# The bias of an attention's output projection: added by TensorE as three bf16 rows, not by GpSimd

## The chip, the cores and the metric

The kernel runs on one NeuronCore of a Trainium2 chip. The metric is the device time of one execution in microseconds (us); shown is the median of three runs. Five engines work side by side and meet only at semaphores: TensorE (PE, with PEld for its weight loads), VectorE (DVE), ScalarE (ACT), GpSimd (POOL) and SyncE (SP, which issues DMAs).

## What is computed

The input is `x` of 16 images by 4 groups by 128 tokens by 256 features, in float32. Three layers follow one another:

```
h = token_mix(x)                       # softmax weights over the 4 groups, weighted sum: 16 x 128 x 256
a = layernorm(h)
q, k, v = a @ W_qkv.T + b_qkv          # 16 heads of 16
p = softmax(causal(q @ k.T) / sqrt(16))
h = h + (p @ v) @ W_o.T + b_o          # the bias in question is b_o
n = layernorm(h)
h = h + moe(n)                         # 64 experts, 6 of them per token, and a shared expert
```

The bias of `v` passes through the softmax unchanged, because the probabilities of a row sum to one. So the kernel adds it as one joint row, `b_o + b_v @ W_o.T`, after the projection. That joint row is what `bo_sb` holds, the same on all 128 partitions.

## The kernel before

The work is tiled by image: 128 tokens lie on the 128 partitions, 256 features in a row. The whole of `h` stays in SBUF as `h_all` (128 x 16 x 256). The program is written out engine by engine. `image_loop` runs a `step(b, par)` on PE, DVE, ACT and POOL for b from -2 or -1 up to 17 or 18, and each step is a software pipeline in which the engines handle different images: image b+3 is mixed and normed by DVE (`a` there; PE and ACT take image b+2 as their `a`), image b+1 gets its V projection, image b its scores and softmax, image b-1 (`cc`) its output projection, residual and second norm, images b-2 (`d`) and b-3 (`e`) their routing to experts and the writing of their rows to DRAM. The order of instructions on each engine is written by hand; every wait is a semaphore. After the loop comes the expert stage, tile by tile (`tile_loop`), and the summing of its results; the change doesn't touch these.

What matters for one step of the loop:

- PE, in its order: `scores()` of image b, the turn of the attention output, V projection (image b+1), transposes, `turn_shift()`, the output projection of image `cc` (line 1252, two products of f32, each run in two passes, into columns 256 to 511 of the bank `psC`), `keyed()` scores, the QKV projection of image b+2, and the products with V (`pv`). All products go through the helper `mm`, so the profile puts them on L1064; the tile names tell them apart.
- DVE, in its order: the first half of the row maxima (`nmax`, L702), the softmax's denominator, the first mixing product, the normalising of the attention output, the second half of `nmax`, `shift_b` (L710, L712), three more mixing instructions (L692), interleaved with the placing (`slot_ix`, L799) and routing (`gsel`, L757) of earlier images, then the residual add of the projection (L905), the norms' statistics, and `apply` (L696), which writes `xn` for the attention or six copies of the normed row for the experts.
- POOL, in its order: the bias add for image b+1 (L406), which waits until DVE has normed that image, the reciprocal root for the norms (`roots`, L381 and L383), and six indirect DMAs that scatter the rows of image b-3 (L398).

The residual add L905 waits for the projection (`proj_done`) and for POOL's bias add of the same image (`bias_added`). Ahead of the loop, DVE mixes and norms images 0 and 1, and its last instruction there, L965, joins the bias and tells POOL (`bias_joined`). `ones_b` is a 128 x 128 tile of bf16 ones that the kernel already uses as stationary operand when it counts rows per expert (L1215). `const_sb` is one table of constants, made on the host and loaded with one DMA.

Of the kernel before, what the change touches and what calls it, by code (L numbers as in the profile page):

```python
# [13 lines left out]
P = 128  # L14
# [36 lines left out]

_at = 0
C_AT = {}
for _name, _n in (("ident", P), ("tri", P), ("tri_t", P), ("pick", GH), ("before", P), ("half", 2), ("ebase", E),
                  ("dest", NB * TOPK), ("spill", 1 + NY), ("upto", E), ("tile", NTAB)):
    C_AT[_name] = (_at, _n)
    _at += _n
# [9 lines left out]
def build(nc, x, w1t, b1, w2t, b2, wqkv, bqkv, wo, bo, gate, gbias, sgu, sd, wexp, const, out):  # L67
# [4 lines left out]
    with ExitStack() as ctx:  # L72
        def sb(name, shape, dt=F32):
            return ctx.enter_context(nc.sbuf_tensor(name, shape, dt))
# [28 lines left out]
        bv_wide = sb("bv_wide", [P, KT, P])  # L103
        wo_sb = sb("wo_sb", [P, KT, D])
        bo_sb = sb("bo_sb", [P, D])
        gate_sb = sb("gate_sb", [P, KT, E])
        gbias_sb = sb("gbias_sb", [P, E])
        gbias_half = sb("gbias_half", [P, E])
# [114 lines left out]
        for name in ("consts_ready", "sum_act", "sum_dve", "tok_chain", "tok_hid", "tok_tanh",  # L223
                     "tok_h", "bv_spread", "bv_projected", "bias_joined", "tok_w", "tok_shift", "tok_exp",
                     "mix_chain", "ln1_done", "xn_transposed", "xnt_ready", "qk_done", "q_ready", "k_ready",
                     "qk_bias", "v_done", "v_ready", "scores_done", "shift_parts", "shift_ready", "shift_turned",
                     "shift_copied", "keyed_done", "exp_done", "pv_done", "ot_ready", "ot_turned", "c2_chain", "o_ready",
                     "o_transposed", "ont_ready", "bias_added", "proj_done", "ln_chain", "x2_ready", "var_ready", "root_ready", "var_eps", "half_set",
                     "x2_transposed", "x2t_ready", "gate_done", "gate_tanh", "g_chain", "score_read", "sel_ready",
                     "pos_done", "key_read", "d_chain", "pool_step", "gu_done", "gu_silu", "sh_chain", "counted",  # L230
                     "shared_done", "h2_ready", "row_ready", "t_chain", "t_count", "t_cum", "t_past", "t_rows",
                     "tab_ready", "xt_done", "xt_ready",
                     "up_done", "silu_done", "h_ready", "h_turned", "ht_ready", "down_done", "pads_zero", "pads_ready", "y_ready",
                     "fin_half", "fin_pair", "fin_ready"):
            S(name)
# [35 lines left out]
        def has(b, lo=0, hi=NB - 1):  # L271
            return not isinstance(b, int) or lo <= b <= hi
# [100 lines left out]
        def _(pool):  # L373
# [16 lines left out]
                roots(n, n + 1, n + 1)  # L390
            pool.wait_ge(S("bias_joined"), 1)

            def step(b, par):
                v, e = b + 1, b - 3

                def scatter(choices):
                    for k in choices:
                        nc.gpsimd.indirect_dma_start(  # L398
                            out=slots_dram,
                            out_offset=bass.IndirectOffsetOnAxis(ap=slot_ix[:, e % NROW, k:k + 1], axis=0),  # L400
                            in_=row_of(e)[:, k, :], in_offset=None).then_inc(scattered[e % NROW], 16)

                if has(v):

                    pool.wait_ge(S("ln1_done"), v + 1)
                    nc.gpsimd.tensor_tensor(h_all[:, v, :], h_all[:, v, :], bo_sb[:], ALU.add).then_inc(  # L406
                        S("bias_added"), 1)
                ahead = TAIL_AHEAD if b == NB else 0
                if ahead:
                    pool.wait_ge(S("row_ready"), e + 1)  # L410
                    scatter(range(ahead))
                if -2 < b <= NB:
                    pool.wait_ge(S("var_ready"), b + 4 if b < 0 else 2 * b + 4 if b <= 12 else b + 16)
                    roots(0 if has(b + 3) else 1, 2 if has(b - 1) else 1, b + 4)
                if has(e):
                    pool.wait_ge(S("row_ready"), e + 1)
                    pool.sem_inc(S("pool_step"), 1)
                    scatter(range(ahead, TOPK))
# [166 lines left out]
        def _(dve):  # L585
# [245 lines left out]
            def step(b, par):  # L831
# [69 lines left out]
                routed(3)  # L901
                if has(cc):
                    dve.wait_ge(S("proj_done"), cc + 1)
                    dve.wait_ge(S("bias_added"), cc + 1)
# [157 lines left out]
        def _(pe):  # L1062
            def mm(*a, **k):
                return nc.tensor.matmul(*a, **k)  # L1064
# [55 lines left out]
            def step(b, par):  # L1120
# [128 lines left out]
                if has(cc):  # L1249
                    pe.wait_ge(S("ont_ready"), cc + 1)  # L1250
                    wait(pe, S("x2_ready"), cc)
                    both(psC[:, D:2 * D], lambda k: ont[:, k, :], lambda k: wo_sb[:, k, :]).then_inc(
                        S("proj_done"), 1)
                if has(b):
                    keyed()
                if has(a):
# [177 lines left out]
```

## Time and profile before

| | |
|---|---|
| median of three runs | 505.59 us (505.51, 505.59, 508.94) |
| profiled execution | 508.18 us, of which 506.4 us lie between its first and its last instruction |
| busy in that span | PE 435.2 us, PEld 335.3, DVE 321.7, POOL 245.9, ACT 215.6 |
| bias adds on POOL (L406) | 16, the first at 25.5 us, the last at 208.6 us |
| first `nmax` of the loop, first one after it | 34.10 us, 48.23 us |

In the tables of the profile PE's time is that of its matrix products, whose ends are modelled. A row of the timeline gives the start in us, the duration in us, the engine, the line, the operation, the tile written and the tiles read, the shape, and how many instructions of a kind are merged in the row; in brackets stands how long the engine was idle before it, and what ended that.
### The profile page before, as it was taken

The numbers are of one execution on the slowest core, as the hardware profiler recorded it, in microseconds if no ns is written. First come the engines' busy times: TensorE is split into PE (matmuls) and PEld (weight loads), VectorE is DVE, ScalarE is ACT, GpSimd is POOL, SyncE is SP. The second block draws the span as 40 slices with busy tenths as digits, with TensorE's granted clock in tenths as the row PEclk, the third lists the DMA queues.
The fourth block names the chain that finished last, engine by engine and source line by source line (L and its number), as shares of the span: only waits on it lengthen the run. The fifth ranks groups of instructions, "written<-read, shape, count | busy, mean of one in ns | idle before, by whom it ended". The sixth has DMA issues, their size and how long they took to land. (4 is left out here: it accounts for less than half of the span.)

```text
span 506.4 us, 13166 instructions
## 1 busy us (share of the span) xinstructions
PE 435.2 (86%) x3950; PEld 335.3 (66%) x3950; DVE 321.7 (64%) x1065; ACT 215.6 (43%) x662; POOL 245.9 (49%) x273
## 2 busy tenths in 40 slices
PE   1667889888989999778369999999999999985995
PEld 1556667676767777454148887888888888862663
DVE  3674789999899998967713443444444444440998
ACT  3254755564545655332004454454444445440000
POOL 1111115766666678766713655665556565661000
PEclk9988999998989999987769999999999999996999
DMA  7999991212111111222235678568577757744997
GB/s 269 337 351 262 277 257 56 72 60 74 65 64 66 64 65 68 83 85 74 104 105 166 194 233 260 173 200 260 174 216 246 226 138 224 212 136 171 377 370 274
DMA packets 56476, 90.00 MB, mean 178 GB/s; under 512 B 7719, under 2 KB 43690, under 8 KB 56400
## 3 DMA queue, kind: packets, MB, share of 16 engines
q1 hardware_dynamic: 44016, 61.69, 40.3%
q0 software_dynamic: 10080, 25.29, 14.0%
q10 hardware_dynamic: 2304, 2.10, 1.2%
q8 instruction: 37, 0.61, 0.6%
q14 instruction: 39, 0.32, 0.2%
HBM read 84.00 MB, written 40.82 MB: 246 GB/s over the span
## 5 line engine op out<-in xcount | busy, mean ns | idle before, releaser
L428 POOL DMA_INDIRECT y_rows<-y,xring x114 | 112.1, 984 | 91.5 <-issue 81.1
L1064 PE MATMUL ps_low<-wring,probt 128*128 x456 | 119.4, 385 | 0.0
L1025 DVE TENSOR_TENSOR probt<-probt,ps_low 128x128 f32<-128x128 f32 x114 | 32.8, 288 | 110.3 <-issue 90.1
L1064 PEld LDWEIGHTS ps_low<-wring,probt 128*128 128x128 f32 x456 | 78.8, 193 | 6.5 <-issue 0.2
L1064 PE MATMUL ps<-wring,probt 128*128 x228 | 68.4, 382 | 0.0
L565 ACT COPY probt<-ps_low 128x256 f32<-128x256 f32 x115 | 42.8, 372 | 50.3 <-PE ps_low L1310 48.7
L398 POOL DMA_INDIRECT slot_rows<-row,slot_ix x48 | 51.5, 1072 | 15.7 <-issue 13.1
L1018 DVE TENSOR_SCALAR y<-ps,xring 128x256 f32<-128x256 f32 x114 | 54.6, 479 | 6.8 <-DMA y_rows<-y,xring 5.3
L398 POOL DMA_INDIRECT slot_rows<-xring,slot_ix x48 | 51.4, 1070 | 14.0 <-issue 13.7
L570 ACT ACTIVATE probt<-ps_low 128x128 f32<-128x128 f32 x114 | 31.7, 278 | 58.1 <-PE ps_low L1064 57.5
L480 ACT ACTIVATE probt<-ps_low 128x512 f32<-128x512 f32 x64 | 33.1, 602 | 43.1 <-PE ps_low L1064 43.1
L1310 PE MATMUL ps_low<-const_sb,xring 128*128 128x128 f32 x230 | 44.9, 277 | 4.2 <-DMA xring<-slot_rows 4.0
L702 DVE TENSOR_REDUCE nmax<-ps_low 128x8 f32<-128x1024 f32 x32 | 39.0, 1217 | 9.3 <-PE ps_low L1064 9.2
L1310 PEld LDWEIGHTS ps_low<-const_sb,xring 128*128 128x128 f32 x230 | 32.5, 143 | 17.4 <-issue 5.1
L381 POOL TENSOR_SCALAR rv<-mv 128x2 f32<-128x2 f32 (+1 forms) x20 | 4.5, 222 | 80.7 <-DVE mv L849 68.3
L1064 PEld LDWEIGHTS ps<-wring,probt 128*128 128x128 f32 x228 | 34.4, 191 | 8.7 <-issue 0.3
L1064 PE MATMUL ps_low<-x_sb,sgu_sb 128*128 128x512 f32 x64 | 32.9, 664 | 7.0 <-issue 7.0
L1064 PE MATMUL ps<-xnt,wqkv_sb 128*128 128x128 f32 x256 | 36.2, 300 | 0.5 <-ACT xnt L513 0.5
L1064 PEld LDWEIGHTS ps<-xnt,wqkv_sb 128*128 128x128 f32 x256 | 33.0, 209 | 3.3 <-issue 2.6
L1297 PE MATMUL ps<-const_sb,probt 128*128 128x128 f32 x114 | 31.3, 275 | 0.8 <-DVE probt L1025 0.8
L559 ACT COPY probt<-ps 128x128 f32<-128x128 f32 x114 | 29.6, 260 | 1.4 <-PE ps L1297 1.3
L1064 PEld LDWEIGHTS ps_low<-x_sb,sgu_sb 128*128 128x128 f32 x64 | 13.5, 216 | 22.9 <-issue 22.6
(184 smaller groups left out, 739.8 us busy)
## 6 DMA issues: line engine op xcount, KB each, us to landing
wring<-wexp SPq DMA_DIRECT2D x115, 384.0 KB
xring<-slot_rows SPq DMA_DIRECT2D x115, 129.0 KB, 2.6
x_sb<-y_rows SPq DMA_DIRECT2D x16, 768.0 KB, 7.0
slot_rows<-pads SPq DMA_DIRECT2D x1, 8256.0 KB
x_sb<-x SPq DMA_DIRECT2D x3, 2048.0 KB, 17.8
slot_rows<-pads SPq DMA_DIRECT2D x5, 516.0 KB
x_sb<-x SPq DMA_DIRECT2D x4, 512.0 KB, 5.3
out<-h_all ACTq DMA_DIRECT2D x16, 128.0 KB, 6.7
```

Of the source, the lines that this page charges most:

```text
L398: nc.gpsimd.indirect_dma_start(out=slots_dram, out_offset=bass.IndirectOffsetOnAxis(ap=slot_ix[:, e % NROW, k:k + 1], axis=0), in_=row_of( ...
L428: nc.gpsimd.indirect_dma_start(out=y_dram, out_offset=bass.IndirectOffsetOnAxis(ap=xring[:, q, TO_AT:TO_AT + 1].bitcast(I32), axis=0), in_ ...
L480: nc.scalar.activation(probt[:, g].rearrange("p a k -> p (a k)"), psQ[g][:], ACT.Exp).then_inc(S("exp_done"), 1)
L559: nc.scalar.copy(ht[:, v % 2, :], ps[4 + v % 2][:, 0:P]).then_inc(S("ht_ready"), 1)
L565: nc.scalar.copy(xt[:, u % 2].rearrange("p a k -> p (a k)"), psT[u % 2][:, 0:D]).then_inc(S("xt_ready"), 1)
L570: nc.scalar.activation(silu[:, t % 2, :], psS[t % 2][:, 0:INTER], ACT.Silu).then_inc(S("silu_done"), 1)
L702: nc.vector.tensor_reduce(nmax[:, two, :], ps_low[:, two, :].rearrange("p g (a k) -> p g a k", a=GH), axis=AX, op=ALU.max, negate=True).th ...
L1018: nc.vector.tensor_scalar(y[:, a, :], ps[6 + v % 2][:, 0:D], xring[:, v % U, W_AT:W_AT + 1], None, ALU.mult).then_inc(S("y_ready"), 1)
L1025: nc.vector.tensor_tensor(hm[:, t % 2, :], silu[:, t % 2, :], psS[t % 2][:, INTER:2 * INTER], ALU.mult).then_inc(S("h_ready"), 1)
L1064: return nc.tensor.matmul(*a, **k)
L1297: nc.tensor.transpose(ps[4 + v % 2][:, 0:P], hm[:, v % 2, :], ident).then_inc(S("h_turned"), 1)
L1310: last = nc.tensor.transpose(psT[u % 2][:, k * P:(k + 1) * P], xring[:, uq, k * P:(k + 1) * P], ident)
```

## The change

POOL's bias adds in the loop are gone, and with them the semaphore `bias_added` on both sides. Ahead of its loop POOL now splits the joint bias into three bf16 terms by ten instructions in a chain: three copies to bf16, two differences in float32, three products with a mask that keeps partition k of term k alone (the new three columns `term` of the constants), and two sums that put the three rows into one tile, `bo_rows`: row 0 holds the first term, row 1 the second, row 2 the third, and the other partitions zero. On PE, each output projection now begins its accumulation with a bf16 product of `ones_b` and `bo_rows`, which adds up the three rows for every token; the two f32 products accumulate on top. Before the first one PE waits once for `bias_rows`. DVE's residual add stays as it is and waits for the projection alone.

```
--- before.py
+++ after.py
@@ -51,7 +51,7 @@
 
 _at = 0
 C_AT = {}
-for _name, _n in (("ident", P), ("tri", P), ("tri_t", P), ("pick", GH), ("before", P), ("half", 2), ("ebase", E),
+for _name, _n in (("ident", P), ("tri", P), ("tri_t", P), ("pick", GH), ("before", P), ("half", 2), ("term", 3), ("ebase", E),
                   ("dest", NB * TOPK), ("spill", 1 + NY), ("upto", E), ("tile", NTAB)):
     C_AT[_name] = (_at, _n)
     _at += _n
@@ -103,6 +103,9 @@
         bv_wide = sb("bv_wide", [P, KT, P])
         wo_sb = sb("wo_sb", [P, KT, D])
         bo_sb = sb("bo_sb", [P, D])
+        bo_rest = sb("bo_rest", [P, 2, D])
+        bo_term = sb("bo_term", [P, 3, D], BF16)
+        bo_rows = sb("bo_rows", [P, D], BF16)
         gate_sb = sb("gate_sb", [P, KT, E])
         gbias_sb = sb("gbias_sb", [P, E])
         gbias_half = sb("gbias_half", [P, E])
@@ -225,7 +228,7 @@
                      "mix_chain", "ln1_done", "xn_transposed", "xnt_ready", "qk_done", "q_ready", "k_ready",
                      "qk_bias", "v_done", "v_ready", "scores_done", "shift_parts", "shift_ready", "shift_turned",
                      "shift_copied", "keyed_done", "exp_done", "pv_done", "ot_ready", "ot_turned", "c2_chain", "o_ready",
-                     "o_transposed", "ont_ready", "bias_added", "proj_done", "ln_chain", "x2_ready", "var_ready", "root_ready", "var_eps", "half_set",
+                     "o_transposed", "ont_ready", "bias_split", "bias_rows", "proj_done", "ln_chain", "x2_ready", "var_ready", "root_ready", "var_eps", "half_set",
                      "x2_transposed", "x2t_ready", "gate_done", "gate_tanh", "g_chain", "score_read", "sel_ready",
                      "pos_done", "key_read", "d_chain", "pool_step", "gu_done", "gu_silu", "sh_chain", "counted",
                      "shared_done", "h2_ready", "row_ready", "t_chain", "t_count", "t_cum", "t_past", "t_rows",
@@ -390,8 +393,24 @@
                 roots(n, n + 1, n + 1)
             pool.wait_ge(S("bias_joined"), 1)
 
+            def split(ins, n):
+                ins.then_inc(S("bias_split"), 1)
+                pool.wait_ge(S("bias_split"), n)
+
+            split(nc.gpsimd.tensor_copy(bo_term[:, 0, :], bo_sb[:]), 1)
+            split(nc.gpsimd.tensor_tensor(bo_rest[:, 0, :], bo_sb[:], bo_term[:, 0, :], ALU.subtract), 2)
+            split(nc.gpsimd.tensor_copy(bo_term[:, 1, :], bo_rest[:, 0, :]), 3)
+            split(nc.gpsimd.tensor_tensor(bo_rest[:, 1, :], bo_rest[:, 0, :], bo_term[:, 1, :], ALU.subtract), 4)
+            split(nc.gpsimd.tensor_copy(bo_term[:, 2, :], bo_rest[:, 1, :]), 5)
+            for k in range(3):
+                split(nc.gpsimd.tensor_scalar(bo_term[:, k, :], bo_term[:, k, :], c("term")[:, k:k + 1], None,
+                                              ALU.mult), 6 + k)
+            split(nc.gpsimd.tensor_tensor(bo_term[:, 0, :], bo_term[:, 0, :], bo_term[:, 1, :], ALU.add), 9)
+            nc.gpsimd.tensor_tensor(bo_rows[:], bo_term[:, 0, :], bo_term[:, 2, :], ALU.add).then_inc(
+                S("bias_rows"), 1)
+
             def step(b, par):
-                v, e = b + 1, b - 3
+                e = b - 3
 
                 def scatter(choices):
                     for k in choices:
@@ -400,11 +419,6 @@
                             out_offset=bass.IndirectOffsetOnAxis(ap=slot_ix[:, e % NROW, k:k + 1], axis=0),
                             in_=row_of(e)[:, k, :], in_offset=None).then_inc(scattered[e % NROW], 16)
 
-                if has(v):
-
-                    pool.wait_ge(S("ln1_done"), v + 1)
-                    nc.gpsimd.tensor_tensor(h_all[:, v, :], h_all[:, v, :], bo_sb[:], ALU.add).then_inc(
-                        S("bias_added"), 1)
                 ahead = TAIL_AHEAD if b == NB else 0
                 if ahead:
                     pool.wait_ge(S("row_ready"), e + 1)
@@ -901,7 +915,6 @@
                 routed(3)
                 if has(cc):
                     dve.wait_ge(S("proj_done"), cc + 1)
-                    dve.wait_ge(S("bias_added"), cc + 1)
                     norm_step(nc.vector.tensor_tensor(image(h_all, cc), image(h_all, cc), psC[:, D:2 * D], ALU.add))
                 routed(4)
                 placed(7)
@@ -1249,8 +1262,12 @@
                 if has(cc):
                     pe.wait_ge(S("ont_ready"), cc + 1)
                     wait(pe, S("x2_ready"), cc)
-                    both(psC[:, D:2 * D], lambda k: ont[:, k, :], lambda k: wo_sb[:, k, :]).then_inc(
-                        S("proj_done"), 1)
+                    if cc == 0:
+                        pe.wait_ge(S("bias_rows"), 1)
+                    mm(psC[:, D:2 * D], ones_b[:], bo_rows[:], start=True, stop=False)
+                    for k in range(KT):
+                        last = mm(psC[:, D:2 * D], ont[:, k, :], wo_sb[:, k, :], start=False, stop=k == KT - 1)
+                    last.then_inc(S("proj_done"), 1)
                 if has(b):
                     keyed()
                 if has(a):
@@ -1397,6 +1414,7 @@
     put("pick", (r == np.arange(GH)[None, :]) | (r == GH + np.arange(GH)[None, :]))
     put("before", p[:, None] < p[None, :])
     put("half", p[:, None] // HD % 2 == np.arange(2)[None, :])
+    put("term", p[:, None] == np.arange(3)[None, :])
     put("ebase", np.arange(E)[None, :] * REGION + P + 1)
     at = (np.arange(NB)[None, :, None] * P + p[:, None, None]) * TOPK + np.arange(TOPK)
     spill = np.full((P, 1 + NY), NOWHERE, np.int32)
```

## Rows read from the trace of the kernel before

**Rows 1.** Attention loop: stretch, us, busy PE, PEld, DVE, ACT, POOL, clock, DMA.

```profile
45.00:211.00 166.00, 149.29 (x2358) 114.35 (x2357) 151.76 (x555) 91.81 (x247) 94.57 (x107) 0.97 0.35 104
```

**Rows 2.** Waits of DVE, 45 to 220 us: us in total, times, longest.

```profile
DVE nmax L702 <- PE ps_low L1064: 7.3, 6, 1.8
```

**Rows 3.** Instructions grouped by line, POOL, 45 to 211 us: busy us, mean ns.

```profile
L406 POOL TENSOR_TENSOR h_all<-h_all,bo_sb 128x256 f32<-128x256 f32 x13 | 9.6, 738 | 0.3
```

**Rows 4.** Single lines, whole span: shortest, median, longest in ns.

```profile
L692 DVE SCALAR_TENSOR_TENSOR h_all<-x_sb,wtok,h_all x48: 469/479/1243, 12.3 to 185.7; 128x256 f32<-128x256 f32 x48
...
L757 DVE TENSOR_SCALAR gsel<-gmr x16: 156/166/718, 64.9 to 238.9; 128x8 f32<-128x8 f32 x16
```

**Rows 5.** Timeline of POOL and DVE, 135 to 137 us.

```profile
135.03 0.96 POOL L398 DMA_INDIRECT slot_rows<-row,slot_ix  x1 [0.30 <-issue]
...
136.01 0.74 POOL L406 TENSOR_TENSOR h_all<-h_all,bo_sb 128x256 f32<-128x256 f32 x1
...
135.58 1.21 DVE L799 TENSOR_SCALAR slot_ix<-key 128x6 int32<-128x6 f32 x1
```

**Rows 6.** Timeline of POOL and DVE near 208.5 us.

```profile
207.60 0.96 POOL L398 DMA_INDIRECT slot_rows<-xring,slot_ix  x1 [0.31 <-issue]
...
208.58 0.73 POOL L406 TENSOR_TENSOR h_all<-h_all,bo_sb 128x256 f32<-128x256 f32 x1
...
208.29 0.42 DVE L757 TENSOR_SCALAR gsel<-gmr 128x8 f32<-128x8 f32 x1
```

**Rows 7.** Timeline of PE and DVE, a step in which DVE waits.

```profile
201.83 0.40 PE L1064 MATMUL ps_low<-tri_b,ident_b 32*32 32x512 bf16 x16
...
202.38 1.23 DVE L702 TENSOR_REDUCE nmax<-ps_low 128x8 f32<-128x1024 f32 x1 [1.43 <-PE ps_low L1064]
```

**Rows 8.** Timeline of PE and DVE, last scores and first `nmax` of three steps.

```profile
105.20 0.40 PE L1064 MATMUL ps_low<-tri_b,ident_b 32*32 32x512 bf16 x16
...
106.28 1.22 DVE L702 TENSOR_REDUCE nmax<-ps_low 128x8 f32<-128x1024 f32 x1
...
116.92 0.40 PE L1064 MATMUL ps_low<-tri_b,ident_b 32*32 32x512 bf16 x16
...
117.78 1.22 DVE L702 TENSOR_REDUCE nmax<-ps_low 128x8 f32<-128x1024 f32 x1
...
142.17 0.40 PE L1064 MATMUL ps_low<-tri_b,ident_b 32*32 32x512 bf16 x16
...
144.13 1.22 DVE L702 TENSOR_REDUCE nmax<-ps_low 128x8 f32<-128x1024 f32 x1
```

**Rows 9.** Timeline of PE, from the shift's turn to the keyed scores.

```profile
51.74 0.23 PE L1064 MATMUL ps<-ident_b,shift_b 128*128 128x128 bf16 x1 [0.40 <-DVE shift_b L712]
...
51.85 1.13 PE L1064 MATMUL ps<-wo_sb,ont 128*128 128x256 f32 x4
...
52.91 0.39 PE L1064 MATMUL ps_low<-qt,kpair 32*128 32x128 f32 x4
```

**Rows 10.** Timeline of POOL and DVE where the loop begins.

```profile
25.51 0.77 POOL L406 TENSOR_TENSOR h_all<-h_all,bo_sb 128x256 f32<-128x256 f32 x1 [0.86 <-DVE bo_sb L965]
...
30.50 0.22 POOL L381 TENSOR_SCALAR rv<-mv 128x1 f32<-128x1 f32 x1 [4.22 <-DVE mv L849]
...
24.69 0.41 DVE L696 TENSOR_SCALAR xn<-h_all,mv,rs 128x256 f32<-128x256 f32 x1 [1.00 <-POOL rs L383]
...
25.73 1.88 DVE L692 SCALAR_TENSOR_TENSOR h_all<-x_sb,wtok,h_all 128x256 f32<-128x256 f32 x3
...
31.40 0.81 DVE L696 TENSOR_SCALAR xn<-h_all,mv,rs 128x256 f32<-128x256 f32 x1 [0.99 <-POOL rs L383]
...
34.10 1.23 DVE L702 TENSOR_REDUCE nmax<-ps_low 128x8 f32<-128x1024 f32 x1 [1.89 <-PE ps_low L1064]
```

**Rows 11.** A stretch (columns of rows 1), and PE's timeline before it.

```profile
121.10:124.50 3.40, 3.40 (x14) 2.60 (x12) 3.40 (x13) 1.50 (x5) 2.79 (x3) 0.50 0.32 115
...
120.75 0.41 PE L1189 MATMUL ps<-const_sb,row 128*128 128x128 f32 x2 [1.59 <-DVE o_sb L726]
```

More of the change, by code:

```diff
@@ L53 @@
 C_AT = {}
-for _name, _n in (("ident", P), ("tri", P), ("tri_t", P), ("pick", GH), ("before", P), ("half", 2), ("ebase", E),
+for _name, _n in (("ident", P), ("tri", P), ("tri_t", P), ("pick", GH), ("before", P), ("half", 2), ("term", 3), ("ebase", E),
                   ("dest", NB * TOPK), ("spill", 1 + NY), ("upto", E), ("tile", NTAB)):
@@ L105, in build @@
         bo_sb = sb("bo_sb", [P, D])
+        bo_rest = sb("bo_rest", [P, 2, D])
+        bo_term = sb("bo_term", [P, 3, D], BF16)
+        bo_rows = sb("bo_rows", [P, D], BF16)
         gate_sb = sb("gate_sb", [P, KT, E])
@@ L227, in build @@
                      "shift_copied", "keyed_done", "exp_done", "pv_done", "ot_ready", "ot_turned", "c2_chain", "o_ready",
-                     "o_transposed", "ont_ready", "bias_added", "proj_done", "ln_chain", "x2_ready", "var_ready", "root_ready", "var_eps", "half_set",
+                     "o_transposed", "ont_ready", "bias_split", "bias_rows", "proj_done", "ln_chain", "x2_ready", "var_ready", "root_ready", "var_eps", "half_set",
                      "x2_transposed", "x2t_ready", "gate_done", "gate_tanh", "g_chain", "score_read", "sel_ready",
@@ L391, in _, with split @@
             pool.wait_ge(S("bias_joined"), 1)
+            def split(ins, n):
+                ins.then_inc(S("bias_split"), 1)
+                pool.wait_ge(S("bias_split"), n)
+            split(nc.gpsimd.tensor_copy(bo_term[:, 0, :], bo_sb[:]), 1)
+            split(nc.gpsimd.tensor_tensor(bo_rest[:, 0, :], bo_sb[:], bo_term[:, 0, :], ALU.subtract), 2)
+            split(nc.gpsimd.tensor_copy(bo_term[:, 1, :], bo_rest[:, 0, :]), 3)
+            split(nc.gpsimd.tensor_tensor(bo_rest[:, 1, :], bo_rest[:, 0, :], bo_term[:, 1, :], ALU.subtract), 4)
+            split(nc.gpsimd.tensor_copy(bo_term[:, 2, :], bo_rest[:, 1, :]), 5)
+            for k in range(3):
+                split(nc.gpsimd.tensor_scalar(bo_term[:, k, :], bo_term[:, k, :], c("term")[:, k:k + 1], None,
+                                              ALU.mult), 6 + k)
+            split(nc.gpsimd.tensor_tensor(bo_term[:, 0, :], bo_term[:, 0, :], bo_term[:, 1, :], ALU.add), 9)
+            nc.gpsimd.tensor_tensor(bo_rows[:], bo_term[:, 0, :], bo_term[:, 2, :], ALU.add).then_inc(
+                S("bias_rows"), 1)
             def step(b, par):
-                v, e = b + 1, b - 3
+                e = b - 3
                 def scatter(choices):
@@ L401, in scatter @@
                             in_=row_of(e)[:, k, :], in_offset=None).then_inc(scattered[e % NROW], 16)
[L403 to L407, printed above, removed]
                 ahead = TAIL_AHEAD if b == NB else 0
@@ L903, in step @@
                     dve.wait_ge(S("proj_done"), cc + 1)
-                    dve.wait_ge(S("bias_added"), cc + 1)
                     norm_step(nc.vector.tensor_tensor(image(h_all, cc), image(h_all, cc), psC[:, D:2 * D], ALU.add))
@@ L1251, in step @@
                     wait(pe, S("x2_ready"), cc)
-                    both(psC[:, D:2 * D], lambda k: ont[:, k, :], lambda k: wo_sb[:, k, :]).then_inc(
-                        S("proj_done"), 1)
+                    if cc == 0:
+                        pe.wait_ge(S("bias_rows"), 1)
+                    mm(psC[:, D:2 * D], ones_b[:], bo_rows[:], start=True, stop=False)
+                    for k in range(KT):
+                        last = mm(psC[:, D:2 * D], ont[:, k, :], wo_sb[:, k, :], start=False, stop=k == KT - 1)
+                    last.then_inc(S("proj_done"), 1)
                 if has(b):
@@ L1399 @@
     put("half", p[:, None] // HD % 2 == np.arange(2)[None, :])
+    put("term", p[:, None] == np.arange(3)[None, :])
     put("ebase", np.arange(E)[None, :] * REGION + P + 1)
```

## The prediction

> **What bounds the kernel now.** I read the busy times of the attention loop first, then who waited for whom in it, then single stretches of the timeline. In the loop over the images VectorE and TensorE are both nearly full: of 166.00 us DVE is busy 151.76 and PE 149.29, POOL 94.57 [rows 1]. So POOL's own time is worth little, and only what it does to DVE or PE counts. A step of that loop closes at the first `nmax` reduction (L702), which needs DVE to be through with the step before and PE to be through with the new scores. DVE stood idle there for PE in 6 steps, 7.3 us in all [rows 2]; the first of these, at 48.23 us, lies ahead of the first product that the change touches, so 5 count. In the other nine steps that follow a projection DVE came late itself. Each step is thus the longer of two paths that start together at `shift_b`: PE's (turn, projection, keyed scores, next QKV, PV, scores) and DVE's (mixing, routing, norms).
>
> POOL's bias add takes 0.738 us, and thirteen of the sixteen lie in this stretch [rows 3]. It isn't free for DVE. Two kinds of DVE instruction whose median times are 0.479 and 0.166 us have single cases of 1.243 and 0.718 us [rows 4], and there are others. Row by row, the long ones end when an add ends: a slot_ix of six columns, begun at 135.58, ended at 136.79, the add at 136.75 [rows 5]. So an add holds a DVE instruction for up to its own length.
>
> **The change part by part.**
>
> *Sixteen adds go.* The holds sit behind `shift_b`, on DVE's path alone, so a hold that goes is worth time only until PE's path ends. A step in which DVE waits shows the lag from the last score to `nmax`: 201.83 + 0.40 to 202.38, 0.15 us [rows 7]. What DVE's `nmax` lies beyond that is the room for a gain. Before the one at 106.28 the room is 106.28 − 105.60 − 0.15 = 0.53, and the hold in the step behind it is the longest of its kind, 1.243 − 0.479 = 0.76. At 144.13 the room is 1.41 and the add of rows 5 takes 0.74 of it. At 117.78 it is 0.31 against 0.55 (0.718 − 0.166); three more steps (168.44, 179.93, 191.43) repeat this pattern, the first with a room of 0.11 [rows 4, 5, 8]. In the last three of the nine no long instruction stands under an add: 0. In the five steps that wait for PE a shorter DVE path only waits longer: 0. Without any new cost: −0.53 −0.74 −3 × 0.31 −0.11 = −2.3 us. DVE's wait for `bias_added` goes too, for nothing: the add ends a step or more before its reader.
>
> *Sixteen bf16 products of 256 columns come.* Each stands after PE's wait for `ont_ready`, between the turn of the shift and the keyed scores. Those start when the projection has been issued (52.91, projection 51.85 to 52.98), and the copy they also need runs beside it [rows 9]. So a product is paid in full on PE's path. No row shows it; the bounds are the spacing behind a bf16 product of half the columns, 51.74 to 51.85, 0.11 us, and one of the four f32 passes of 256 columns, 1.13 / 4 = 0.28. Its weights are the bf16 `ones_b`, as in the first kind, so I take 0.13, near that row. A gain below zero is excluded, PE gets only more to do. Its price: 5 waiting steps × 0.13, the same from each of the four rooms that limited a gain and from the small one, nothing from the step at 144.13 (its room is far larger than the hold) and nothing from the three without a hold, whose rooms of about 0.2 or more cover it; 2 × 0.13 for the last two projections. With 0.13 the six steps give −0.40 −0.74 −3 × 0.18 + 0.02 = −1.66, the waiting and last ones +0.91: **−0.75 us**. With 0.11: −1.0. With 0.28: +1.2.
>
> The Trainium skill (TensorE: Matmul & The Clock Gate, section "Back-to-back issue gap") gives 262 cycles for 256 columns, 0.109 us at the upper clock; by it the sum would be −1.0.
>
> *Ten POOL instructions come at the start.* They begin where the first add began, 25.51, and what is queued behind them is the root for image 2 (L381, at 30.50), for which DVE's `xn` waits [rows 10]. Four have two inputs, as the add: 0.738 each. Six have one: between 0.22, a scalar operation on two columns, and 0.738; I take the middle, 0.48, as neither end is near. Each but the first waits for the one before; 0.1 for each such gap is an estimate (an add follows a scatter after 0.02 without a wait, rows 6). The chain takes 4 × 0.738 + 6 × 0.48 + 1.0 = 6.8 us and ends at 32.3; the bounds are 30.0 (0.22, gaps of 0.02) and 33.9 (0.738). The root's result and `xn` follow 0.9 and 0.41 later (30.50 to 31.40, and `xn` alone, at 24.69; the 0.81 at 31.40 has a hold in it): 33.6. The first `nmax` starts at 34.10, because PE's scores are late, after 1.89 us of idling. So the cost is **0**, covered by that wait; with the upper bound, and an estimated 0.8 for DVE instructions that get in between, it is 1.9. It can't gain, since PE sets the 34.10 [rows 6, 10].
>
> *The rest.* PE's wait for `bias_rows` falls at the first projection, 51.85, some 20 us behind the chain [rows 9]: 0. Behind it would be queued everything of PE, so it would cost only if the chain took 20 us more. Three constant columns are 1.5 KB on a 0.45 MB load: 0. No DMA is moved; POOL's six scatters per step stay where they are, and what stood between them and the next root only gets shorter.
>
> **Sum.** The profiled execution took 508.18 us around its span of 506.4; it would take 507.4. It is 2.6 above the median shown, 505.59; the same 0.75 off that is 504.8.
>
> **The rivals.**
>
> *All holds are time* (if DVE alone set the steps). Thirteen adds at the middle hold of 0.55 are 7.2 us: 498.4. For it: DVE's 91% busy share. Against it: five steps that wait for PE, and rooms of 0.3 in most others [rows 1, 2, 8]. 4%.
>
> *Slower: the ten-instruction chain keeps DVE out.* The mixing of image 2 (25.73, three instructions of the kind that is held) would then wait not for one POOL instruction but for the end of all ten. From 25.73 to the end of `xn`, 32.21, are 6.5 us, of which two holds of about 0.4 would go (1.88 against 3 × 0.479, 0.81 against 0.41); so 5.7 us of DVE's work would follow the chain's end, and it decides as soon as that end lies behind 34.10 − 5.7 = 28.4. With 32.3 `nmax` starts at 38.0, 3.9 us late; with 33.9 it is 5.5 late, and more if bf16 is slow on POOL. Time: 508.7 to 510.3, over 510.6 if the chain lasts 0.3 us beyond my bound [rows 4, 10]. For it: at 135.58 slot_ix was held through the end of a scatter (135.99) and the add that began 0.02 later [rows 5]. Against it: at 208.29 another got through in just such a gap, ending at 208.71 with the scatter over at 208.56 and the add from 208.58 on [rows 6]. In the chain every instruction waits for the one before, so its gaps are wider. 12%.
>
> The Trainium skill (SBUF — State Buffer, "Who interferes with whom") says that VectorE and GpSimd share a port pair as an exclusive lock held for one whole instruction, the earlier one winning. By that rule the rival's hold would be one instruction each time and it would have no chance; rows 6 agree, rows 5 don't quite.
>
> *The new work costs its upper bounds*: product 0.28 (+1.2) and chain 1.9, +3.1 us: 508.7. Only the f32 pass speaks for it. 10%.
>
> *The clock decides.* In 121.10 to 124.50 the granted clock was 0.50, the lower level of 1.2 GHz, after PE had stood 1.59 us waiting for DVE's `o_sb` [rows 11]. A stretch like it costs PE up to half its 3.4 us. With waits moved by tenths, one more or one fewer is possible: 1.7 either way, 503.1 or 506.5. 16%.
>
> **How the numbers follow.** The forecast has 58%: 504.8. The range takes in the product's and the chain's bounds and one clock stretch: 502.9 to 508.7; it leaves out the first rival and most of the second, about 15%. I call 1%, 5 us, the least that a measurement of this kernel can tell from no change. Faster by more: 5%, the first rival and a little. Slower by more: 6%, half of the second. Within 1%: 89%.
>
> **What would show it.** Right: no long slot_ix, gsel or mixing instruction any more; DVE waits for PE at `nmax` in ten or more steps instead of 6, with more than 7.3 us in total; the product 0.1 to 0.15 us behind the turn; the first `nmax` still near 34.1 with an idle time before it. Wrong: a mixing instruction of several us at 25.7 (the second rival); steps shorter by 0.5 us throughout (the first); keyed scores 0.28 later behind the turn (the third).

## The result, and the profile of the changed kernel

The changed kernel took **502.27 us** (median of 20 runs, 498.63 to 507.3) against 505.55 us (20 runs, 501.86 to 509.45): ratio 0.9935, 95% interval 0.9908 to 0.9961, so 3.3 us faster, between 2.0 and 4.7. The prediction was 504.8 with a range from 502.9: the sign and "within 1%" held, the size didn't, and the time lies 0.6 us below the range. A second comparison on one other chip gave 502.96 (12 runs) against 504.50 (17 runs), ratio 0.9942 (0.9906 to 0.9977); that median lies just inside the range. The ratios leave out runs more than 1.5% above the fastest of their kernel; the clock table below takes all of them, and there the difference of the means is 1.95 us (± 1.1).

The profiled execution of the changed kernel took 500.24 us around a span of 498.2, 2.0 under its median, while the one of before stood 2.6 over its own. The two pages alone would therefore give 7.9 us, more than twice what is there to explain.

First the loop in the changed kernel, as in [rows 1] (us, busy PE, PEld, DVE, ACT, POOL, clock, DMA):

```profile
45.00:211.00 166.00, 149.85 (x2418) 114.55 (x2418) 147.86 (x558) 92.90 (x252) 86.84 (x97) 0.99 0.34 105
```

DVE's and POOL's busy times fell (151.76 to 147.86, 94.57 to 86.84), PE's did not. DVE's waits for PE at `nmax` between 45 and 220 us, against [rows 2] (us in total, times, longest):

```profile
DVE nmax L716 <- PE ps_low L1077: 8.7, 10, 2.2
```

Single lines of DVE, whole span, shortest/median/longest in ns, against [rows 4]:

```profile
L706 DVE SCALAR_TENSOR_TENSOR h_all<-x_sb,wtok,h_all x48: 468/480/773, 12.0 to 183.1; 128x256 f32<-128x256 f32 x48
...
L771 DVE TENSOR_SCALAR gsel<-gmr x16: 156/165/380, 65.4 to 235.1; 128x8 f32<-128x8 f32 x16
...
L813 DVE TENSOR_SCALAR slot_ix<-key x16: 159/167/368, 75.6 to 237.7; 128x6 int32<-128x6 f32 x16
```

The longest mixing instruction fell from 1243 to 773 ns (it is at the start, beside the new chain), the longest `gsel` from 718 to 380, and the slot_ix of 1.21 us [rows 5] is gone. What is left over the median is some 0.2 us, under scatters.

PE's timeline from the turn to the keyed scores, against [rows 9] (start, us, instruction):

```profile
52.20 0.23 PE L1077 MATMUL ps<-ident_b,shift_b 128*128 128x128 bf16 x1 [1.11 <-DVE shift_b L726]
52.30 0.27 PE L1077 MATMUL ps<-bo_rows,ones_b 128*128 128x256 bf16 x1
52.40 1.03 PE L1077 MATMUL ps<-wo_sb,ont 128*128 128x256 f32 x4
53.36 1.06 PE L1077 MATMUL ps_low<-qt,kpair 32*128 32x128 f32 x28
```

From the turn to the keyed scores it is 1.16 us; before it was 1.17 here [rows 9], and 1.13 in its undisturbed steps. The product is there, 0.10 us long in spacing, but what follows it moved by only 0.03 to 0.04.

The start of the loop, POOL and DVE, against [rows 10]:

```profile
25.19 0.45 POOL L400 CAST bo_term<-bo_sb 128x256 bf16<-128x256 f32 x1 [0.84 <-DVE bo_sb L978]
...
28.36 3.00 POOL L406 TENSOR_SCALAR bo_term<-bo_term,const_sb 128x256 bf16<-128x256 bf16 x3
...
32.19 0.67 POOL L409 TENSOR_TENSOR bo_rows<-bo_term 128x256 bf16<-128x256 bf16 x1
32.83 0.23 POOL L384 TENSOR_SCALAR rv<-mv 128x1 f32<-128x1 f32 x1
...
25.43 1.84 DVE L706 SCALAR_TENSOR_TENSOR h_all<-x_sb,wtok,h_all 128x256 f32<-128x256 f32 x3
...
33.74 0.41 DVE L710 TENSOR_SCALAR xn<-h_all,mv,rs 128x256 f32<-128x256 f32 x1 [3.67 <-POOL rs L386]
34.07 1.22 DVE L716 TENSOR_REDUCE nmax<-ps_low 128x8 f32<-128x1024 f32 x1
...
32.97 0.39 PE L1077 MATMUL ps_low<-tri_b,ident_b 32*32 32x512 bf16 x16
```

The chain ran to 32.86 (32.3 was forecast), DVE's mixing went on beside it (1.84 us, before 1.88), `xn` ended at 34.15 (33.6 was forecast) and `nmax` started at 34.07 (34.10). But the idle time before `nmax` is gone: PE's last score ended at 33.36, and with the lag of 0.15 [rows 7] `nmax` could have started at 33.51. Here DVE arrives 0.56 us after PE, and there is no cover left.

Last, a low stretch of the clock in the loop (a stretch in which the granted clock reads 0.50) and the wait before it, against [rows 11]:

```profile
75.90:79.10 3.20, 3.20 (x40) 2.41 (x42) 3.20 (x14) 0.00 (x0) 0.00 (x0) 0.50 0.02 5
```

```profile
73.84 0.41 PE L1202 MATMUL ps<-const_sb,row 128*128 128x128 f32 x2 [1.27 <-DVE o_sb L740]
```

This trace has one of them inside the loop; that of before has two, the one of [rows 11] and one from 148.4 on.

### The profile page after: what moved, and what is told of

The parts are those of the page before. It is cut to its first block, busy times and chain, and to the rows that moved or that the text cites. A ratio compares the mean times of both kernels' runs of the same rounds, so it can differ in the third digit from the quotient of the medians.

```text
span 498.2 us, 13176 instructions
## 1 busy us (share of the span) xinstructions
PE 432.2 (87%) x3966; PEld 333.7 (67%) x3966; DVE 315.1 (63%) x1065; ACT 215.8 (43%) x662; POOL 240.2 (48%) x267
## 3 DMA queue, kind: packets, MB, share of 16 engines
q1 hardware_dynamic: 44016, 61.69, 40.6%
## 4 chain that ended last, share of the span: by engine, by line
PE 22%; issue 9%; POOL 7%; DMA 7%; DVE 4%; SPq 1%; POOLq 1%; DVEq 0%
PE ps_low L1077 12%; POOL y_rows L442 6%; PE ps L1077 6%; DMA x_sb<-y_rows 4%; PE ps_low L1327 3%; DMA y_rows<-y,xring 2%; PE ps L1314 2%; DVE x_sb L1055 1%; DVE h_all L1060 1%; DVE x_sb L1065 1%; DVE x_sb L1072 1%; DMA xring<-slot_rows 1%; DMA slot_rows<-xring,slot_ix 1%; SPq L359 0%; POOLq L442 0%
## 5 line engine op out<-in xcount | busy, mean ns | idle before, releaser
L579 ACT COPY probt<-ps_low 128x256 f32<-128x256 f32 x115 | 42.8, 372 | 48.7 <-PE ps_low L1327 48.5
L500 ACT ACTIVATE kpair<-ps,bk_half,const_sb 128x128 f32<-128x128 f32 x64 | 24.4, 486 | 6.9 <-PE ps L1077 6.9
```

Of the source, the lines that this page charges most:

```text
L579: nc.scalar.copy(xt[:, u % 2].rearrange("p a k -> p (a k)"), psT[u % 2][:, 0:D]).then_inc(S("xt_ready"), 1)
```

## The experiments

Two theories stood against each other. **Holds**: the adds held DVE, and the 3.3 us are holds gone, net of the products. **Clock**: the change moves PE's waits, and so the time that it spends at the lower clock level.

**The bias left out.** No adds, no products, no chain; the output lacks the bias.

```
-  pool: tensor_tensor(h_all[v], h_all[v], bo_sb, add)      (x16)
-  dve.wait_ge(bias_added, cc + 1)
```

> Leaves the attention's output bias out: neither POOL's adds nor the bf16 products nor the chain that splits the bias. Holds theory (the gain is the DVE instructions that no longer wait for POOL; the product costs nearly nothing, 0.01 to 0.04 us from the shift's turn to the keyed scores): like the changed kernel or up to 0.5 us faster, 501.5 to 502.5; no DVE instruction under an add, nmax waits for PE in most steps. Clock theory (the products keep TensorE busier, so it falls less often to the lower clock): without them no gain, about 505, and as many low stretches in the loop as before.

Measured: 500.54 us (8 runs), ratio 0.9909 (0.9877 to 0.9941). PE from the projection to the keyed scores, whose distance is 1.06 as in [rows 9]:

```profile
50.93 1.13 PE L1058 MATMUL ps<-wo_sb,ont 128*128 128x256 f32 x4 [0.25 <-ACT ont L513]
51.99 1.17 PE L1058 MATMUL ps_low<-qt,kpair 32*128 32x128 f32 x32
```

That is 1 us below the range of the holds theory and far below the clock theory's 505; the trace has no low stretch in mid loop either, where the clock theory expected as many as before. So the whole bias costs the old kernel some 4.6 us (4.1 by the means), and the change recovers about half of that by the means. From here on "the loop" is the time from the second `nmax` to the sixteenth, counting the first one of each step. It took 160.13 us here, and 160.9 in three of the four traces of the changed kernel that have no low stretch there (160.5 in the fourth): the products cost 0.8 us there, about 0.05 a step.

**The adds put back.** The changed kernel, with POOL's adds on a tile that nobody reads, and DVE's wait.

```
+  pool.wait_ge(ln1_done, v + 1)
+  tensor_tensor(bo_rest[v % 2], h_all[v], bo_sb, add).then_inc(bias_added, 1)   (POOL)
+  dve.wait_ge(bias_added, cc + 1)
```

> The changed kernel with POOL's sixteen adds put back, onto a tile that nobody reads, with DVE's wait for them; the products and the chain stay, so the bias is added once, by TensorE. Holds theory: the gain is gone, 505 to 506.5, long slot_ix, gsel and mixing instructions are back under the adds. Clock theory: 502 to 503, as the changed kernel.

Measured: 505.51 us (12 runs), ratio 1.0015 (0.9985 to 1.0046): the whole gain is gone. The long instructions are back (shortest/median/longest, ns):

```profile
L711 DVE SCALAR_TENSOR_TENSOR h_all<-x_sb,wtok,h_all x48: 473/480/1232, 12.2 to 184.7; 128x256 f32<-128x256 f32 x48
...
L776 DVE TENSOR_SCALAR gsel<-gmr x16: 156/184/730, 67.2 to 238.2; 128x8 f32<-128x8 f32 x16
```

The adds are what counts, but not by the holds alone: here the chain and an add stand ahead of the root, and the first `nmax` starts at 35.34, 1.3 us later than in the changed kernel. A second trace:

> The changed kernel with the adds put back, a second trace. If the waits that the holds bring let the clock fall, low stretches between 52 and 210 us in this or that trace, as in the kernel before; if the sixteen products keep it up, again none, and 162.4 us from the second nmax to the sixteenth.

It took 505.29 us, with the first `nmax` at 35.39; its loop took 162.48 us (162.40 in the first). Neither trace has a low stretch between 52 and 208 us. So without a change of the clock the adds cost the loop 1.5 us (162.4 against 160.9).

**Five products for one.** Four more bias products in each step, overwritten.

```
+  for _ in range(4):
+      mm(psC[:, D:2 * D], ones_b[:], bo_rows[:], start=True, stop=True)
```

> The changed kernel with the bias product issued five times per projection, each overwriting the last, so that the result is the same. If the first one is hidden behind the load of the f32 weights and the loop is now bound by PE in every step: 0.11 us for each further one, turn to keyed scores 1.17 + 0.43 = 1.6 us, in all 16 x 0.43 = 6.9 us, 509. If VectorE still bounds most steps: the rooms of 0.3 us swallow most, 2 to 3 us, 505. Clock theory: TensorE busier, fewer low stretches, below 505.

Measured: 507.05 us (12 runs), ratio 1.0046 (1.0016 to 1.0076). PE, turn to keyed scores:

```profile
52.45 0.72 PE L1077 MATMUL ps<-bo_rows,ones_b 128*128 128x256 bf16 x5 [0.32 <-ACT ont L532]
53.01 1.03 PE L1077 MATMUL ps<-wo_sb,ont 128*128 128x256 f32 x4
53.97 1.17 PE L1077 MATMUL ps_low<-qt,kpair 32*128 32x128 f32 x32
```

From the first product to the keyed scores it is 1.52 us, with one it was 1.06 (52.30 to 53.36): 0.115 for each further product in this step. In the later steps, where nothing waits, the turn lies 1.60 us ahead of the keyed scores with five products and 1.16 with one: 0.11 each. The Trainium skill (TensorE: Matmul & The Clock Gate, "Back-to-back issue gap") has 262 cycles for 256 columns, 0.109 us at the upper clock. The further ones agree. The first one does not cost that, only some 0.03 to 0.04, since the projection's f32 weights now load while it runs. Those loads, in the kernel before and in the changed one:

```profile
51.85 0.73 PEld L1064 LDWEIGHTS ps<-wo_sb,ont 128*128 128x128 f32 x4
...
52.30 0.73 PEld L1077 LDWEIGHTS ps<-wo_sb,ont 128*128 128x128 f32 x4
```

Before, they start with the projection itself (51.85); in the changed kernel they start with the bias product, 0.10 us ahead of the projection (52.40), and from the projection to the keyed scores it is 0.96 us in place of 1.06. DVE's waits at `nmax` rose to 12.8 us in 12 steps: with five products PE sets nearly all steps, and the loop takes 165.75. The time lies between the two that were expected, 505 and 509, and there is no low stretch in mid loop.

**The chain behind the first root.**

```
     for b in ...:  # POOL's loop
         ... root of step b ...
+        if b == -1:
+            split_bias()          # the ten instructions, moved here
```

> The changed kernel with POOL's ten instructions behind the first root of the loop instead of ahead of it. In the changed kernel xn of image 2 waited 3.67 us for that root and the first nmax began 0.5 us later than PE's scores allowed. Holds theory: the first nmax 0.5 us earlier, xn not held, in all 0 to 0.5 us faster, 501.8 to 502.3; three mixing instructions at 37 us are held instead, at no cost. If the chain at the start cost nothing: the same time as the changed kernel.

Measured: 502.77 us (12 runs), ratio 0.9951 (0.9925 to 0.9978). DVE's start has its idle time back:

```profile
31.23 0.47 DVE L714 TENSOR_SCALAR xn<-h_all,mv,rs 128x256 f32<-128x256 f32 x1 [1.07 <-POOL rs L386]
33.94 1.23 DVE L720 TENSOR_REDUCE nmax<-ps_low 128x8 f32<-128x1024 f32 x1 [2.25 <-PE ps_low L1081]
```

In the median this can't be told from the changed kernel. It answers a later question, below.

**More traces of both kernels.** Times of one kernel spread over 7 us, so one trace each was too little.

> The kernel before, unchanged, for a second trace. Open is why the change gave 3.3 us where the holds, with a product of 0.04 us, make 1.9. If the rest is the clock: again two low stretches between the second nmax and the sixteenth, and that part of the loop again about 165 us. If the rest is chance in one trace: no low stretch there, and 162.5 us.

> The kernel before, unchanged, for a third trace; as for the second. Clock: two low stretches in the loop, 165 us from the second nmax to the sixteenth. Chance: none, 162.5 us.

> The changed kernel, unchanged, for a second trace. Clock: at most one low stretch between the second nmax and the sixteenth, 160.5 to 162 us. Chance: the number of low stretches there scatters from 0 to 2 as in the kernel before.

> The changed kernel, unchanged, for a third trace; as for the second: 160.5 to 162 us from the second nmax to the sixteenth by the clock theory, 0 to 2 low stretches by chance.

They took 505.41 and 509.10 (before), 499.46 and 498.39 (changed). Both of before have low stretches in mid loop, the longer one four (columns of [rows 1]):

```profile
110.20:113.40 3.20, 3.20 (x36) 2.38 (x38) 3.20 (x13) 0.14 (x1) 2.74 (x3) 0.50 0.26 88
123.80:127.00 3.20, 3.20 (x36) 2.44 (x38) 3.20 (x9) 0.08 (x1) 0.98 (x2) 0.50 0.13 46
147.70:154.30 6.60, 6.36 (x63) 5.50 (x63) 6.60 (x24) 1.50 (x5) 3.71 (x5) 0.50 0.22 80
175.00:178.20 3.20, 3.20 (x24) 2.37 (x27) 3.20 (x14) 0.48 (x3) 2.59 (x3) 0.50 0.27 97
```

Its loop took 169.21 us. Both of the changed kernel have none there, and 160.93 and 160.92. Each low stretch in mid loop, in either kernel, begins within 2.1 us of the end of a wait of 1.25 to 2.3 us that PE made for DVE's `o_sb`; but not every such wait is followed by one (1.78 us in no_bias, 1.57 in adds_kept, 1.42 in five traces of the changed kernel). That led to a test of the clock by itself.

**PE's wait filled.** The kernel before, adds and holds as they were, with three bf16 products that nobody reads ahead of PE's wait for `o_sb`; late_filled is the version with the chain behind the root, filled in the same way.

```
   # PE, after wait_ge(x2_ready, d + 1), ahead of the wait for o_ready
+  for _ in range(3):
+      mm(psO[:, P:3 * P], ones_b[:], pick_b[:, 0:2, :].rearrange("p a k -> p (a k)"),
+         start=True, stop=True)
```

> The kernel before, adds and holds included, with three more bf16 products per step that write a free part of a PSUM bank while PE waits for o_sb; their result is not read. Clock theory (in the kernel before, PE's waits for DVE let its clock fall to the lower level in mid loop, and that costs about 2 of the 3.3 us): no low stretch between 52 and 210 us, 162.1 us from the second nmax to the sixteenth, 502.5 to 504. Holds alone (the low stretches are chance and cost nothing on the average): 505 to 506, as the kernel before, with low stretches as there.

> The same kernel again for a second trace. Clock theory: again no low stretch between 52 and 210 us and 162.1 us of loop. Holds alone: one to five low stretches, 163 to 169 us, as in the three traces of the kernel before.

> The changed kernel with the splitting behind the first root and the three products in PE's wait for o_sb: the version that the experiments point to. The changed kernel hardly falls to the lower clock in the loop any more, so both theories expect little there, 160.9 us from the second nmax to the sixteenth. The clock theory expects a gain at the low stretches at the loop's two ends (46 us, 211 to 232 us), up to 1.5 us: 500.5 to 502. Holds alone: 502 to 503, as the changed kernel.

Measured: before_filled **501.00 us** (12 runs), ratio 0.9926 (0.9897 to 0.9956); a second trace 500.50; late_filled **499.31 us** (6 runs), ratio 0.9897 (0.9848 to 0.9945), the fastest version of the study. PE in before_filled, with the fill at 119.75:

```profile
119.75 0.49 PE L1064 MATMUL ps<-pick_b,ones_b 128*128 128x256 bf16 x3
121.42 0.44 PE L1189 MATMUL ps<-const_sb,row 128*128 128x128 f32 x2 [1.18 <-DVE o_sb L726]
```

and its loop, where the clock reads 1.00 throughout (0.98 in this stretch of the first trace of before):

```profile
52.00:208.00 156.00, 145.33 (x2338) 111.76 (x2337) 145.85 (x539) 89.40 (x243) 95.28 (x107) 1.00 0.32 97
```

PE has more to do, no hold is gone, and the kernel is as fast as the changed one. Its loop took 162.13 and 161.67 us, that of before 163.27 to 169.21. Where before_b has no low stretch, its steps are as long as those of before_filled, within 0.05 us from the second `nmax` on. So the three products change nothing there by themselves; what they take away is the low stretches. This is the clock by itself. The steps also give a price for one such stretch: the step that holds the one of before_b took 12.86 us where before_filled takes 11.71, 1.15 us more, and in before_d two steps in a row were longer, by 2.4 us together.

**Longer runs of the changed kernel.** Its 20 first runs go from 498.6 to 507.3, and none of the traces so far was from the upper half.

> The changed kernel again, for traces from the slower half of its runs (9 of the 20 first ones took 504 to 507.3 us, the three traced ones 498.4 to 500.2). Clock theory: where such a run is caught, it has low stretches between 52 and 210 us as the kernel before has them, and 163 us or more from the second nmax to the sixteenth. Rival: that part takes 160.9 us there too, and the time is lost in the expert stage, which the change leaves alone.

> As after_d: in a run above 504 us low stretches in the loop (clock theory), or 160.9 us of loop and a longer expert stage (rival).

> As after_d: in a run above 504 us low stretches in the loop (clock theory), or 160.9 us of loop and a longer expert stage (rival).

> The kernel before, a fourth trace. Clock theory: low stretches between 52 and 210 us again, at least one, as in each of its three traces. Rival: none.

They took 507.06, 499.47, 501.89 and 503.55 us. The longest, after_d, has one low stretch in mid loop and a loop of 162.64 us, between the two that were expected. It lost most of its time where the loop starts: PE's scores were ready early, `nmax` was not, since it stood behind the chain, and PE waited 2.18 us for `shift_b`.

**Both kernels with the clock of every run.** To tell the clock's share from the rest, one more comparison.

> The changed kernel itself, with the granted clock of every timed run on both sides, on one chip. Over 130 timed runs of this study, within one kernel, a microsecond less at the lower clock went with 0.33 us less time (low time worked out as (1 - mean clock) x 2 x span). So far the changed kernel had 46.3 us of it on average and the kernel before, on other chips, 48.3. Theory: the clock explains only some 0.7 us of the difference and about 1.1 to 1.9 us stay at an equal clock (holds gone, net of a product at 0.04 us). Rival: the difference of 3.3 us is mostly clock. The theory expects mean clocks within 0.004 of each other and a difference of 1.5 to 3.0 us, of which 1 to 2 remain after 0.33 us per microsecond of low time is taken off; the rival expects a mean clock higher by 0.006 or more and under 0.7 us left at an equal clock.

Measured: 502.96 (12 runs, mean clock 0.9548) against 504.50 (17 runs, 0.9515), ratio 0.9942 (0.9906 to 0.9977). Its trace, at 506.51 us, repeats after_d. First the wait and the first two `nmax` (timelines of PE and DVE), then the stretches:

```profile
37.24 0.29 PE L1077 MATMUL ps<-ident_b,shift_b 128*128 128x128 bf16 x1 [2.20 <-DVE shift_b L726]
...
34.15 1.22 DVE L716 TENSOR_REDUCE nmax<-ps_low 128x8 f32<-128x1024 f32 x1
...
51.75 1.22 DVE L716 TENSOR_REDUCE nmax<-ps_low 128x8 f32<-128x1024 f32 x1 [0.95 <-PE ps_low L1077]
```

```profile
37.20:43.80 6.60, 6.21 (x78) 5.38 (x79) 2.91 (x10) 2.33 (x5) 0.80 (x2) 0.50 1.09 286
47.40:54.00 6.60, 6.60 (x48) 4.82 (x48) 3.49 (x12) 1.26 (x3) 0.00 (x0) 0.50 1.09 334
```

The first step took 17.60 us. In before_d, where PE's scores were early too, `nmax` began at 33.42, PE waited 0.66 us, and that step took 13.31:

```profile
36.52 0.23 PE L1064 MATMUL ps<-ident_b,shift_b 128*128 128x128 bf16 x1 [0.66 <-DVE shift_b L712]
```

**The sum at an equal clock.** Of 159 timed runs the mean granted clock is known. Since the levels are 1.2 and 2.4 GHz, (1 − clock) × 2 × span is a run's time at the lower one. Within one kernel a microsecond less of it goes with 0.36 us less time (r = 0.79); [rows 11]'s bound, half, is in line with that. This is a correlation, and the kernels taken one by one give 0.12 to 0.53. With it the difference of the means to before (65 runs, three chips, 504.73 us, 48.4 us low) parts into two:

| kernel | runs | low, us | difference | 0.36 × low | at an equal clock (95%) |
|---|---|---|---|---|---|
| changed | 32 | 45.9 | −1.95 | −0.90 | −1.05 ± 0.6 |
| no_bias | 8 | 44.3 | −4.06 | −1.50 | −2.56 ± 0.75 |
| adds_kept | 12 | 45.0 | +0.90 | −1.24 | +2.14 ± 0.7 |
| five_products | 12 | 40.6 | +2.33 | −2.83 | +5.16 ± 0.5 |
| chain_late | 12 | 46.5 | −2.35 | −0.71 | −1.64 ± 0.6 |
| before_filled | 12 | 39.0 | −3.92 | −3.40 | −0.52 ± 0.7 |
| late_filled | 6 | 38.1 | −5.20 | −3.70 | −1.49 ± 0.7 |

The two theories each hold a part: before_filled gains by the clock alone, no_bias mostly at an equal clock, and the changed kernel about half and half; with the lowest and the highest of the slopes the clock's part in the changed kernel is 0.3 or 1.3 us. The last expectation's theory holds (clocks 0.0033 apart, 2.4 us between the means, 1.1 left at an equal clock), its rival does not.

## Why the prediction was right in kind and wrong in size

**The holds: right in sum, two steps by luck.** All long DVE instructions that lay under an add are gone, and only the rooms were won. Without low stretches the loop takes 162.1 us with the holds (before_filled) and 160.9 without them (after_b), both with the second `nmax` at 48.5; the rows are the second and the sixteenth `nmax` of each:

```profile
48.56 1.22 DVE L702 TENSOR_REDUCE nmax<-ps_low 128x8 f32<-128x1024 f32 x1
...
210.69 1.23 DVE L702 TENSOR_REDUCE nmax<-ps_low 128x8 f32<-128x1024 f32 x1 [1.02 <-PE ps_low L1064]
...
48.52 1.22 DVE L716 TENSOR_REDUCE nmax<-ps_low 128x8 f32<-128x1024 f32 x1
...
209.46 1.23 DVE L716 TENSOR_REDUCE nmax<-ps_low 128x8 f32<-128x1024 f32 x1 [1.86 <-PE ps_low L1077]
```

That is 1.2 us, net of the products; no_bias against before_filled gives 2.0 for the holds without the products, where the sum had 2.3. DVE waits for PE in ten steps, 8.7 us in all, as the prediction asked (ten or more, over 7.3). The rival "all holds are time" (7.2 us) is out.

But "−0.74" at 144.13 and nothing at 157.0 were read from steps that low stretches had lengthened. The room of 1.41 at 144.13 follows the stretch at 121.1, and PE was late at 157.0 after the one at 148.4. In before_b, which has neither, the tenth `nmax` has a room of 0.41 and the eleventh one of 0.57. The ninth to the eleventh in before_b, then in after_b:

```profile
131.67 1.21 DVE L702 TENSOR_REDUCE nmax<-ps_low 128x8 f32<-128x1024 f32 x1
...
143.76 1.22 DVE L702 TENSOR_REDUCE nmax<-ps_low 128x8 f32<-128x1024 f32 x1
...
155.51 1.22 DVE L702 TENSOR_REDUCE nmax<-ps_low 128x8 f32<-128x1024 f32 x1
...
130.09 1.21 DVE L716 TENSOR_REDUCE nmax<-ps_low 128x8 f32<-128x1024 f32 x1
...
142.13 1.22 DVE L716 TENSOR_REDUCE nmax<-ps_low 128x8 f32<-128x1024 f32 x1
...
153.36 1.22 DVE L716 TENSOR_REDUCE nmax<-ps_low 128x8 f32<-128x1024 f32 x1 [0.17 <-PE ps_low L1077]
```

The step that should have given 0.74 gave 0.05 (12.09 to 12.04), and the one that should have given nothing gave 0.52 (11.75 to 11.23). That the sum is near 2.3 all the same is luck.

**The product: mis-sized.** "So a product is paid in full on PE's path" and "I take 0.13": that failed. It is on the path, but moved the keyed scores by 0.03 to 0.04 us, less than the lower bound of 0.11, because the projection's weights load beside it, which the spacing behind another bf16 product [rows 9] does not show. The prediction's own sum contains the product twelve times; with 0.04 it comes to −2.31 + 12 × 0.04 = −1.8 us in place of −0.75. Over the whole loop the products cost 0.8 us (160.13 to 160.9), half of the forecast twelve times 0.13, and more than their 0.04 a step: two of the fourteen steps, at 176 and 187 us in after_b, are 0.22 longer than in no_bias, and why was not found. Further products behind the first did cost 0.11.

**The start: the forecast of the chain held, its cover did not always.** Its end was 0.56 us later than forecast: the three scalar products on bf16 took 1.0 us each, above the bound of 0.738. The rival "the chain keeps DVE out" is wrong: mixing took 1.84 us beside it, DVE getting in between POOL's instructions. The Trainium skill (SBUF — State Buffer, "Who interferes with whom") has the engine that issues first get the shared port pair for the whole instruction. This row agrees. The cost of **0** failed, though, since "PE sets the 34.10" rested on one execution. PE's scores come at other times in others. In the seven traces of the changed kernel the first `nmax` came 0.4 to 0.6 us later than the scores allowed in three and 1.9 us in two (after_d, after_g); in two the chain was covered. In after_d and after_g `nmax` came at 34.2, 0.8 us behind before_d, and with the low stretches that followed the second `nmax` came 5.0 us behind it (51.75 against 46.73). chain_late, whose first `nmax` waits for PE again, is 0.6 ± 0.7 us better than the change at an equal clock, which the runs do not settle.

**The clock: the step that put the time outside the range.** "With waits moved by tenths, one more or one fewer is possible: 1.7 either way" took low stretches for chance of either sign, with 16%. The size of 1.7 for one lies between the two that were measured (1.15 and 2.4); the "either way" failed. All four traces of before have one to four of them in mid loop, 7.7 us on the average; of seven of the changed kernel three have one and four have none, 1.5 us on the average; the eight traces of the variants have none. From 50 to 210 us PE waited 13.1 to 14.5 us for `o_sb` in the four traces of before, in the changed kernel (us in total, times, longest)

```profile
PE ps L1202 <- DVE o_sb L740: 11.3, 13, 1.4
```

and 7.9 in before_filled. So the change had a side to which it would push the clock, and the prediction had the row for it. Over the runs this is worth some 0.9 us; without it the median would be 503.2, inside the range. Which part of the change does it is not shown: in no_bias, without holds and without products, PE waited 13.3 us for `o_sb`, and in adds_kept, with both, 12.8, nearly as in before, and neither has a low stretch. What before alone has is five or six waits of 1.25 us or more in each trace; the changed kernel has one to three, no_bias and adds_kept three, before_filled none.

Together: at an equal clock the runs give −1.05 ± 0.6 (the forecast was −0.75). The loop without low stretches gives −1.2, holds −2.0 and products +0.8, and the start takes some of it back. With −0.9 from the clock that is −1.95, at the small end of the first comparison's interval. The −3.3 of that comparison against −1.5 in the medians of the second shows how far the median of one set still moves.

**Open.** Which runs PE's early scores fall in, and what decides it, was not found. The traces also differ behind the loop, where nothing was changed and for which the prediction had no term. From the sixteenth `nmax` to the end the four of before took 291.1 us on the average (290.0 to 293.2) and the seven of the changed kernel 288.7 (287.5 to 290.2). A low stretch that begins between 449 and 458 us lasts 10.2 us in all four of before and in no_bias, 6.8 us in all seven and in the other variants. So part of the clock's share may lie there and not in the loop; why was not tried. And adds_kept has less low time than before though its holds are back and PE waited 12.8 us for `o_sb` in it; why stays open.

## What to carry to other kernels

An engine that holds another is worth what the held path lacks against the next one, so read the room step by step before summing holds. Then ask which side the change pushes PE's waits to, because where waits are followed by a low clock they can be worth as much as the path itself; three products that nobody reads, put into such a wait, gained 3.9 us here in the means without touching anything else. And a cover or a room read from one execution, like the 1.89 us before the first `nmax` or the 1.41 at 144.13, has to be seen in several, and in one without low stretches, before a step is costed by it.

## What the runs showed of the hardware

- A bf16 product of 256 columns ahead of an f32 projection cost 0.03 to 0.04 us, four more behind it 0.11 each.
- POOL took 1.0 us for 128x256 bf16 times one scalar per partition (2.09 for two in chain_late), but 0.40 to 0.47 for a cast of the same tile from f32 and 0.67 to 0.73 with two inputs.
- A wait of PE of 2.2 us at the loop's start was followed by two low stretches of 6.8 us (after_d, after_g); waits of 0.28 to 1.9 us there, in the other traces, by stretches of 3.4 us.
- A low stretch of 3.4 us in mid loop lengthened the steps it fell into by 1.15 us in before_b and by 2.4 us in before_d.
